# The skip term of a scan layer through flips of a scaled copy instead of matmuls with diagonal matrices

## What is computed

```python
def step(h, ins):
    a_t, bx_t, c_t, xc_t = ins
    h = a_t * h + bx_t
    y_t = jnp.einsum('bds,bs->bd', h, c_t) + D_param * xc_t
    return (h, y_t)
```

## Time and profile before

| | before |
|---|---|
| median of 3 runs | 1153.08 us |
| lowest, highest | 1148.04, 1153.71 us |
| profiled execution | 1156.35 us, span 1154.6 us |
| TensorE busy | 1034.4 us (90%) |
| VectorE busy | 1059.7 us (92%) |
| ScalarE busy | 1005.4 us (87%) |
| GpSimd busy | 991.4 us (86%) |
| mean granted TensorE clock | 0.979 of full speed |

### The profile page before, as it was taken

One profiled execution on the slowest core, in us unless ns is written; L12 is line 12 of the kernel. 1 busy time (PEld: TensorE's weight loads), 2 busy tenths in 40 slices (PEclk: granted clock), 3 DMA queues, 4 the chain that ended last, 5 costly groups with the idle time before them and its releaser, 6 DMA issues. The chain is left out here.

```text
span 1154.6 us, 18311 instructions
## 1 busy us (share of the span) xinstructions
PE 1034.4 (90%) x5831; PEld 734.4 (64%) x5831; DVE 1059.7 (92%) x1475; ACT 1005.4 (87%) x2195; POOL 991.4 (86%) x608
## 2 busy tenths in 40 slices
PE   4676788999999999998999999999999999999996
PEld 2454566676766666675676767576666767666665
DVE  2999998999999999999999999999999999999531
ACT  6778897999998999999999999999999999998543
POOL 0577797999979999998999999998989999999854
PEclk9688998999999999999999999999999999999999
DMA  6544535356563645565364545556354555535122
GB/s 168 209 156 158 174 112 184 117 216 187 210 177 122 217 140 215 164 220 176 134 218 162 196 139 221 177 191 206 127 191 138 218 189 213 177 127 191 57 87 58
DMA packets 84113, 194.51 MB, mean 168 GB/s; under 512 B 17288, under 2 KB 47936, under 8 KB 67632
## 3 DMA queue, kind: packets, MB, share of 16 engines
q1 hardware_dynamic: 84016, 193.33, 49.1%
HBM read 179.14 MB, written 5.77 MB: 160 GB/s over the span
## 5 line engine op out<-in xcount | busy, mean ns | idle before, releaser
L943 POOL TENSOR_TENSOR read<-state,bc_all 128x1024 f32<-128x1024 f32 x256 | 604.5, 2364 | 64.7 <-DVE state L813 57.7
L813 DVE TENSOR_TENSOR_SCAN state<-decay,drive_bank 128x512 f32<-128x512 f32 (+1 forms) x464 | 594.1, 1315 | 4.0 <-POOL read L943 2.3
L763 ACT ACTIVATE decay<-delta,a_neg 128x252 f32<-128x252 f32 x1024 | 423.7, 495 | 1.0
L805 DVE TENSOR_TENSOR drive_bank<-dx_bank,bc_all 128x512 f32<-128x512 f32 (+1 forms) x496 | 331.5, 702 | 5.7 <-DMA bc_all<-bc_dram 5.0
L372 PE MATMUL y_bank<-ident,read 128*128 128x128 f32 x2048 | 275.4, 280 | 26.3 <-POOL read L943 26.2
L372 PEld LDWEIGHTS y_bank<-ident,read 128*128 128x128 f32 x2048 | 239.2, 145 | 84.2 <-POOL read L943 54.0
L988 POOL TENSOR_TENSOR hid<-gu,comb_all 128x512 f32<-128x512 f32 (+1 forms) x136 | 165.0, 1214 | 15.6 <-DVE gu L903 7.9
L363 PEld LDWEIGHTS down_bank<-down_w,hid 128*128 128x128 f32 x1024 | 129.2, 192 | 25.0 <-issue 22.7
L363 PE MATMUL down_bank<-down_w,hid 128*128 128x128 f32 x1024 | 136.1, 276 | 1.5 <-POOL hid L988 1.5
L363 PE MATMUL bank<-x2T,gate_w 128*128 128x512 f32 (+1 forms) x272 | 133.4, 580 | 3.5 <-DVE gu L903 2.4
L363 PE MATMUL bank<-x2T,up_w 128*128 128x512 f32 (+1 forms) x272 | 132.4, 571 | 2.8 <-DVE gu L903 1.4
(11 more groups left out here) (130 smaller groups left out, 1392.5 us busy)
## 6 DMA issues: line engine op xcount, KB each, us to landing
bc_all<-bc_dram SPq DMA_DIRECT2D x128, 1024.0 KB, 6.7
comb_all<-comb_dram SPq DMA_DIRECT2D x240, 128.0 KB, 3.1
x_in<-in_x_dram SPq DMA_DIRECT2D x15, 256.0 KB, 5.3
ctx_in<-in_ctx_dram SPq DMA_DIRECT2D x15, 256.0 KB, 8.3
k_pair<-k_pair SPq DMA_DIRECT2D x30, 128.0 KB, 2.1
q_pair<-q_pair SPq DMA_DIRECT2D x30, 128.0 KB, 4.8
out_dram<-y_out SPq DMA_DIRECT2D x15, 256.0 KB, 3.1
comb_all<-comb_dram SPq DMA_DIRECT2D x32, 64.0 KB, 2.6
```

Source lines behind the costliest of these rows:

```text
L763: done = e.activation(seqs(decay_t[j % DECAYS][:, i, h, :])[:, :, 1:T], seqs(delta[c % 2][:, h, sub * SUB:(sub + 1) * SUB])[:, :, 1:T], AC ...
L805: e.tensor_tensor(drive_bank[:, a:b, :, :], dx_bank[:, :, :].unsqueeze(1).to_broadcast(shape), bc_all[group % BC_BUFS][:, 0, PAIR * i + a: ...
L813: e.tensor_tensor_scan(states(state_t[j % STATE_BUFS], a, b), states(decay_t[j % DECAYS], a, b), states(drive_bank, a, b), 0.0, ALU.mult, ...
L943: e.tensor_tensor(read_t[j % READS][:, :, :, :], state_t[j % STATE_BUFS][:, :, :, :], bc_all[group % BC_BUFS][:, 1, PAIR * i:PAIR * (i + 1 ...
```

## The change

Each half now opens its sums with four flips of a scaled copy. ScalarE computes `xd = D_param * xc`, two activations Copy over 128x256 with the column of `d_param` as scale, into one buffer `xd` [128, 2, 256]; TensorE flips its four blocks into `y_bank`. The copy waits for `xc`, and until the seed of the half before has been taken (`y` of its first step). The seed waits for the new semaphore `xd` in place of `mamba_dve`. The new stage is placed at -6 and 37 (0 in the last chunk). `d_diag` and its two products on VectorE are gone. Nearly all places of the other stages change as well, most by a few ticks.

```diff
 AT = {
-    "xT_mm": [(-46, -45)],
-    "tap_mm": [(-39, -39)],
+    "xd": [(-6, 0), (37, 1)],
+    "xT_mm": [(-49, -46)],
+    "tap_mm": [(-40, -39)],
...
-    "r1_var_mm": [(84, 71)],
+    "r1_var_mm": [(80, 71)],
     "score_mm": [(97, 88)],
-    "combT_mm": [(136, 128)],
+    "combT_mm": [(136, 124)],
...
-    "xc0": [(-35, -36)],
-    "xc1": [(-33, -34)],
+    "xc0": [(-37, -34)],
+    "xc1": [(-35, -26)],
...
-    "q_rot": [(84, 79)],
-    "q": [(86, 82)],
+    "q_rot": [(86, 78)],
+    "q": [(90, 82)],
...
     "z_mm": [(9, 27), (37, -40)],
-    "gate_z": [(12, 26), (41, 27)],
-    "y_gated": [(40, 55), (69, -18)],
-    "yT_mm": [(60, 64), (69, 12)],
+    "gate_z": [(9, 25), (41, 27)],
+    "y_gated": [(40, 61), (70, -18)],
+    "yT_mm": [(56, 64), (70, 12)],
...
     "down_mm": [
-        (142, 148), (157, 184), (160, 208), (168, 227), (177, 231), (183, 255), (184, 278), (190, 288), (193, 304)],
+        (144, 163), (155, 193), (160, 216), (168, 229), (177, 237), (182, 255), (182, 272), (190, 282), (192, 304)],
...
-EXP_AT = [-9, -9, -5, -4, 1, 3, 4, 15, 18, 22, 27, 33, 33, 43, 45, 53]
-LAST_EXP_AT = [-10, -10, -6, -3, 4, 5, 23, 25]
+EXP_AT = [-10, -9, -6, -4, 1, 3, 4, 15, 19, 23, 25, 31, 31, 41, 45, 53]
+LAST_EXP_AT = [-10, -10, -6, -3, 4, 13, 23, 25]
...
                     if n == 0:
-                        w.wait_ge(S["mamba_dve"], 1)
+                        w.wait_ge(S["xd"], half + 1)
                         w.wait_ge(S["y_gated"], half)
                         for q in range(SUB_BLOCKS):
-                            cols = slice(sub * SUB + q * P, sub * SUB + (q + 1) * P)
                             for h in range(HALVES):
-                                mm(y_bank[:, q, h * P:(h + 1) * P], xc[c % 2][:, h, cols], d_diag[:, h, :],
-                                   start=h == 0 and q == 0, stop=False)
+                                flip(y_bank[:, q, h * P:(h + 1) * P], xd[:, h, q * P:(q + 1) * P],
+                                     start=h == 0 and q == 0, stop=False)
...
+                for c, sub in due(tick, "xd"):
+                    w.wait_ge(S["early_consts"], 16 * 11)
+                    w.wait_ge(S["xc"], at(c, 1, HALVES))
+                    w.wait_ge(S["y"], steps_before(c) + SUB_STEPS * (sub - 1) + 1)
+                    for h in range(HALVES):
+                        done = e.activation(xd[:, h, :], xc[c % 2][:, h, sub * SUB:(sub + 1) * SUB], ACT.Copy,
+                                            scale=d_param[:, h:h + 1])
+                    done.then_inc(S["xd"], 1)
...
                     w.wait_ge(S["early_consts"], 16 * 11)
-                    for h in range(HALVES):
-                        e.tensor_scalar(d_diag[:, h, :], ident[:, :], d_param[:, h:h + 1], 1.0, ALU.mult, ALU.mult)
                     w.wait_ge(S["a_exp"], 1)
```

## The result

The changed kernel takes 1168.55 us (median of 4 runs, 1163.91 to 1170.44) against 1152.24 us before: ratio 1.0137, 95% interval 1.0119 to 1.0156. The forecast was 1153.0 us, no change, with a range up to 1160.5; the kernel is slower than that. The profiled execution took 1169.05 us (span 1167.3).

What follows compares the result with a forecast made beforehand. VectorE was taken to bound the long middle, between a head and a TensorE-bound tail. Terms +2.0 + 0 + 0 - 0.7 - 0.5 - 0.9 = -0.1 us gave 1153.0 us from a 1153.08 median, range 1146.5 to 1160.5.

Steps and rivals of the forecast that it cites:

- the head: Start of the kernel: `a_exp` between two Silus adds table loads, ScalarE 2.8 us later, VectorE +2.0 us (0 to 2.9).
- the copies: ScalarE's 64 activations `xd`, 0.40 us each, 26 us in all, said to fit in its idle time: 0 on the path.
- the hand-over of `dx_bank`: Middle chunks: `xc1` ahead of `dx_bank` delays a drive 0.5 us, next `gu` leaves 0.14; taken as 0 (-3 to +2).
- the end of the scans: Last chunks: moved `q`, `down_mm` and exponentials, followed to `retout_mm` of chunk 15: -0.5 us (-2.7 to +1.5).
- The ceiling of 2.9 us: High end of the +2.0 us term for the kernel's start, if every bit of the delay arrives.
- there ScalarE waits for TensorE anyway: Cover for both copies of a chunk: 0.77 us of waiting at `ret_copy`, 4.9 us per chunk behind the other.
- TensorE's 14.4 us: Seeds of `y_bank`: flips replacing `d_diag` products save TensorE 14.4 us, on no path in the middle, so worth 0.
- The rival of 8 us: ScalarE late at the `dx_bank` hand-over, each of 15 chunks losing 0.5 us: +8 us, 1161 us, chance 0.12.
- The 2.9 us wait: VectorE's single wait of `gate_z` for the sums in `y_bank`, shortened by TensorE's saving: -0.7 us (0 to -2.9).
- The tail: After the scans: `combT_mm` of chunk 16 comes behind the second down tile, not the third: -0.9 us (0 to -1.5).
- The signs that I had named: Checks including VectorE idle 14 to 20 us in the middle, first scans 2 us later, three more table loads.
- VectorE's waits for ScalarE pass 8 us: Sign in the middle (100 to 1060 us) that would show the forecast wrong.

Runs made afterwards that it cites:

- e15_second_only: Kernel before with copies and flips for each chunk's second half only, first halves keeping the `d_diag` products, old places: ratio 1.0012.
- e8_first_twice: e2_mechanism with an idle second copy in front of each `xd` of a chunk's first half: ratio 1.0126 to the kernel before.
- e16_copies_only: Kernel before with the 64 copies `xd` added, written to a tile nobody reads, and the `d_diag` products kept: ratio 1.0033.
- e2_mechanism: Changed kernel's copies `xd` and flips alone, with all other places as in the kernel before: ratio 1.0021 to the kernel before.
- e7_k_copy: e2_mechanism with `k_copy` one place earlier on ScalarE (tick 64 in place of 66): ratio 1.0163 to the kernel before.
- e13_before_again: The kernel before, unchanged, run again under another name for a second profile: ratio 1.0011, profiled execution 1154.27 us.

## Why the prediction was wrong, step by step

The sum of -0.1 us came from small terms that nearly cancel. What failed is the size of the head's term (2.0 for 4.4), three places put at nothing (the copies, the hand-over of `dx_bank`, and the queue of SyncE, which was not looked at), and the end of the scans, forecast as a gain. The new places carry 11.2 of the 15.8 us by themselves, the mechanism 2.4.

**The head, +2.0 forecast, 4.2 to 4.4 measured.** The mechanism was right, the size was not. The step carried ScalarE's 2.8 us along, but took TensorE's next products at their old durations. After the longer wait they took 0.9 us more each, twice, and `dx_bank` ended at 33.81 in place of the 31.0 worked out; 0.7 us more are `xc0`, which starts at 13.97 in this profile in place of 13.30. The ceiling of 2.9 us ("if every bit arrives") left both out. The Trainium skill, "TensorE: Matmul & The Clock Gate", Part 1, section "What's actually happening", has matmuls at half rate while TensorE is cold. The durations here fit it (1.93 for 1.06 us), but the recorded clock of the stretch, 1.00, does not show it, so this reason for the 0.9 us is not shown.

**The copies, 0 forecast.** Their spacing was right. The failed step is "there ScalarE waits for TensorE anyway". It was checked for one of the two copies, at `ret_copy`, and holds there by the trace (`e15_second_only`). For the other I set 73 us of idle time, all of ScalarE's in the stretch and not only what stands behind that copy, against 23 us of work. That copy delays `k_copy`, on which a DMA, GpSimd and its reads hang. `e8_first_twice` shows that nothing absorbs it. In time it is 2.4 us (0.9 to 3.8).

**TensorE's 14.4 us, worth 0.** Right: the seeds' rows are 13.9 us less, and `e16_copies_only` cannot be told from `e2_mechanism`.

**The hand-over of dx_bank, 0 forecast (-3 to +2).** The slip of 0.5 us was named, but it was said that the next `gu` would take it up. `gu`'s 0.28 us goes, and two waits of 0.57 us together come. `tap_mm`, going ahead, was taken as a gain; it stood ahead of `up_mm`, which `gu` needs. By repair: 1.5 us for `xc1`, within the interval. The rival of 8 us, 7.5 of them for this place, was on the right side and too dear.

**The queue of SyncE, not in the sum at all.** One tick, 160 to 159, changed which of two transfers waits behind the other: 25.4 us of SyncE's waiting, 3.1 us by the time, of which VectorE's waits show 0.5. I compared the orders of ScalarE and TensorE tick by tick, and of SyncE only in the head.

**The 2.9 us wait, -0.7 forecast.** The wait is 1.2 us in the second profile. The changed kernel does not have it, but a `gu` waits 1.3 us for TensorE in the same chunk: no gain is to be seen.

**The end of the scans, -0.5 forecast (-2.7 to +1.5).** The delay of step 253's decays was foreseen; TensorE's `up_mm` then waits 1.26 us for the `silu`, and a `gu` 0.49 us in place of 1.1. `xc1` of chunk 16 at -26, behind the copies, was not. The last chunk's places together cost 4.9 us up to the last scan, of which the tail gives 3.9 back; by the times they cost 2.0, within the interval.

**The tail, -0.9 forecast.** Open. The two traces that differ in these places alone differ by 1.0 us, but so do two traces with the same places.

**The signs that I had named.** "VectorE's waits for ScalarE pass 8 us" did not come: they read 3.9 us (2.3 of them for `silu`). But 3.6 us stand under "DVE state" and are waits for ScalarE's `dx_bank`, and 3.7 under "issue" are waits for TensorE. The idle time, 25.4 us against the 14 to 20 named, was the better sign. The first scan came 4.1 us late where 2 were named, and there are four more table loads (181 for 177), not three.

The ledger of 15.8 us: head, last chunk and `xc1` 8.5 together (4.4, 2.0 and 1.5 alone), `comb_load` 3.1, mechanism 2.4; 1.8 us remain, within the intervals. Clear of their intervals are the 8.5 together, the head, and the mechanism; the 3.1 are so barely. No kernel here beats the one before.

## What to carry to other kernels

When an order is written out by hand to the last 0.03 us, idle time of an engine is no cover. Ask of each piece of work that is pushed back how long its result lay ready before the bound engine took it, and follow the first consumer across DMA and other engines. Compare the queues one by one, the DMA queue too, and count a step as moved even when one tick changes. And test repairs together: `tap_mm` put back alone cost 9.4 us, and together with `down_mm` nothing that can be measured.

## What the runs showed of the hardware

**VectorE can be held for a whole GpSimd instruction.** In `e7_k_copy`, 11 of the 15 `weighted` over 128x192 took 2.3 to 2.5 us, each ending 0.2 us after GpSimd's product of 128x1024 that ran beside it. The four that started when this product had ended or not begun took 0.36 us, and so did all but one in the two profiles of the kernel before (2.54 us in `e13_before_again`, started 0.02 us after the product). Where `weighted` started 0.03 us ahead, GpSimd's product took 2.56 us instead of 2.4. Drives and `gu`, with one operand in PSUM, run beside GpSimd's reads at 0.67 to 0.69 us. The Trainium skill, "SBUF — State Buffer", section "Who interferes with whom", says that a VectorE instruction with two SBUF inputs contends with a GpSimd instruction that reads SBUF, and, of VectorE's two-port modes, that the one which comes second blocks fully. This trace agrees with the first, and shows the second for `weighted` too: it ended only after GpSimd's product wherever it started after it. The old order has the router's work on VectorE exactly where GpSimd waits 2.09 us for the swap; so that wait was no waste either.

**TensorE after a wait.** After 3.83 us of waiting in the head the same products took 1.8 times as long, at a recorded clock of 1.00; after 1.96 and 1.43 us of waiting near 1035 us an up product took 2.08 us instead of 1.02, and there the record shows 0.62. So the column showed the slowness in one of two such stretches; the durations of one shape, compared, show it in both.
